# K's transposes by DMA instead of TensorE, from the second sequence on

## The reference

```python
h = layernorm(x, ln_g, ln_b)
q = (h @ Wq).reshape(B, S, H, DH).transpose(0, 2, 1, 3)
k = (h @ Wk).reshape(B, S, H, DH).transpose(0, 2, 1, 3)
q = l2norm(q) * q_scale
k = l2norm(k) * k_scale
logits = jnp.einsum('bhid,bhjd->bhij', q, k) * QK_SCALE
logits = jnp.where(causal, logits, NEG_INF)
attn = jax.nn.softmax(logits, axis=-1)
```

## Time and profile before

| | |
|---|---|
| median of 3 runs | 1125.51 us (1121.51 to 1126.7) |
| the profiled execution's own time | 1120.17 us |
| its span, first to last instruction | 1118.4 us |
| mean granted TensorE clock | 0.986 |
| busy: PE / DVE / ACT / POOL | 96% / 86% / 70% / 25% |
| share of the chain that ended last: PE / DVE / ACT | 89% / 4% / 2% |

### The profile page before, as it was taken

How to read it: one execution, slowest core, us unless ns; L and a number is a source line. 1 busy time by engine, 2 the same in 40 slices (tenths; PEclk the granted TensorE clock), 3 DMA queues, 4 the chain that set the end, 5 groups by cost and what they waited for, 6 DMA issues and landing times.

```text
span 1118.4 us, 27576 instructions
## 1 busy us (share of the span) xinstructions
PE 1075.0 (96%) x10435; PEld 912.2 (82%) x10435; DVE 959.6 (86%) x2543; ACT 778.9 (70%) x1772; POOL 277.7 (25%) x328
## 2 busy tenths in 40 slices
PE   4877999999999999999999999999999999999997
PEld 1664888888888888888888888888888888888897
DVE  8988798898988989898898989889898888988763
ACT  5873948668595876859677594867759587685653
POOL 2340314224031231404123140412403132140200
PEclk9995999999999999999999999999999999999999
DMA  7010000000000000000000000000000000000000
GB/s 210 7 39 10 2 11 7 1 16 1 11 7 11 6 2 16 1 11 6 6 11 2 11 7 11 6 1 16 2 11 6 11 7 6 6 6 1 7 2 10
DMA packets 18722, 14.60 MB, mean 13 GB/s; under 512 B 2408, under 2 KB 16160, under 8 KB 18592
## 3 DMA queue, kind: packets, MB, share of 16 engines
q1 hardware_dynamic: 17680, 12.76, 3.8%
q10 hardware_dynamic: 912, 0.09, 0.1%
HBM read 10.75 MB, written 2.10 MB: 11 GB/s over the span
## 4 chain that ended last, share of the span: by engine, by line
PE 89%; DVE 4%; issue 3%; ACT 2%; POOL 1%; SPq 0%; DMA 0%; POOLq 0%; DVEq 0%; ACTq 0%
PE O L565 19%; PE O L468 14%; PE S L484 5%; PE U L547 5%; PE U L548 5%; PE U L549 5%; PE J L382 5%; PE S L449 4%; PE J L343 4%; PE U L449 4%; PE S L404 4%; PE J L344 3%; PE J L345 3%; PE S L400 3%; PE O L475 2%
## 5 line engine op out<-in xcount | busy, mean ns | idle before, releaser
L777 ACT ACTIVATE hid<-U,b1c 128x256 f32<-128x256 f32 x512 | 200.5, 474 | 174.8 <-PE U L549 174.7
L565 PE MATMUL O<-w2s,hid 128*128 128x128 f32 x2048 | 251.1, 276 | 0.0
L565 PEld LDWEIGHTS O<-w2s,hid 128*128 128x128 f32 x2048 | 238.6, 192 | 2.9
L928 POOL TENSOR_SCALAR_AFFINE_SELECT P<-P 128x512 f32<-128x512 f32 x128 | 85.0, 664 | 618.6 <-ACT P L750 618.5
L468 PEld LDWEIGHTS O<-Vx,P 128*128 128x128 f32 x1536 | 188.0, 192 | 30.2 <-issue 14.3
L468 PE MATMUL O<-Vx,P 128*128 128x66 f32 x1536 | 188.6, 273 | 3.6 <-POOL P L928 2.0
L1198 DVE TENSOR_TENSOR_SCAN st<-aexp,u 128x256 f32<-128x256 f32 x256 | 178.8, 698 | 0.4 <-issue 0.3
L920 POOL TENSOR_TENSOR raw<-raw,nr 128x512 f32<-128x512 f32 x124 | 132.8, 1097 | 134.9 <-DVE nr L1066 134.9
L1208 DVE SCALAR_TENSOR_TENSOR y<-st,bc,y 128x256 f32<-128x256 f32 x240 | 133.5, 556 | 8.5
L547 PE MATMUL U<-h2h,w1h 128*128 128x256 f16 x480 | 130.9, 273 | 0.0
L549 PE MATMUL U<-h2h,w1l 128*128 128x256 f16 x480 | 130.9, 273 | 0.0
(11 more groups left out here) (204 smaller groups left out, 2048.0 us busy)
## 6 DMA issues: line engine op xcount, KB each, us to landing
xin<-in_L_attn_x SPq DMA_DIRECT2D x16, 128.0 KB, 2.1
xres<-in_L_attn_x SPq DMA_DIRECT2D x16, 128.0 KB, 2.3
hid<-in_L_ffn_w SPq DMA_DIRECT2D x2, 1024.0 KB, 6.5
out_dram<-fin SPq DMA_DIRECT2D x16, 128.0 KB, 1.8
raw<-in_L_ffn_Wq SPq DMA_DIRECT2D x1, 512.0 KB, 4.7
raw<-in_L_ffn_Wk SPq DMA_DIRECT2D x1, 512.0 KB, 6.4
raw<-in_L_ffn_Wv SPq DMA_DIRECT2D x1, 512.0 KB, 7.4
wos<-in_L_ffn_Wo SPq DMA_DIRECT2D x1, 512.0 KB, 11.4
```

The costliest lines, as they stand in the source:

```text
L565: last = mm(O[e % 2][:, t * P:(t + 1) * P], hid[:, e % 2, m, t * P:(t + 1) * P], w2s[:, e * FC + m, :], start=(m == 0), stop=(m == FC - 1))
L777: fn(hid[:, e % 2, f % FC, :], U[q % 2][:, m * SEQ:(m + 1) * SEQ], ACT.Gelu_apprx_tanh, bias=b1c[:, f:f + 1], scale=1.0 / WS).then_inc(gel ...
```

## The change

From the second sequence on, K is split into its halves in token order, into two new tiles `Kh` and `Kl`, and the halves are turned from there by DMA transposes of 128x128 that SyncE issues, into `KTh` and `KTl`. Q goes the old way. Sequence 0 is left as it was. The core of the diff:

```diff
+KT = 2 * T * 16
...
+        Kh = sb("Kh", [P, T, HD], F16)
+        Kl = sb("Kl", [P, T, HD], F16)
...
+        kt_high = [sem(f"kt_high{q}") for q in range(NP // 2)]
+        kt_low = [sem(f"kt_low{q}") for q in range(NP // 2)]
...
+        def turn_bank(s, n):
+            return J[n % 2] if s == 0 else J[n // 2 % 2]
...
+            def turn_keys(s, quarter, low):
+                if quarter == 0 and not low:
+                    sp.wait_ge(st_ready, s * NP)
+                if low:
+                    sp.wait_ge(t_lo, s * NL + 2 * quarter + 2)
+                else:
+                    sp.wait_ge(t_hi, s * NL + 2 * quarter + 2)
+                src, dst, done = ((Kl, KTl, kt_low) if low else (Kh, KTh, kt_high))
+                for p in (2 * quarter, 2 * quarter + 1):
+                    for t in range(T):
+                        sp.dma_start_transpose(dst[:, p, t * P:(t + 1) * P], src[:, t, p * P:(p + 1) * P]
+                                               ).then_inc(done[quarter], 16)
...
                 if older:
                     store_out(i - 2)
+                if new:
+                    for quarter in range(NP // 2):
+                        turn_keys(i + 1, quarter, False)
+                        turn_keys(i + 1, quarter, True)
...
             def scores_for_max(s, p):
-                pe.wait_ge(t_hi, s * NL + 2 * (p // 2) + 2)
+                if s == 0:
+                    pe.wait_ge(t_hi, 2 * (p // 2) + 2)
+                else:
+                    pe.wait_ge(t_hi, s * NL + 2 * (p // 2) + 1)
+                    pe.wait_ge(kt_high[p // 2], s * KT)
...
+                if p % 2 == 0 and s > 0:
+                    pe.wait_ge(kt_low[p // 2], s * KT)
...
                     if new and m in TURN_AT:
                         turn_qk(i + 1, TURN_AT[m])
-                        turn_qk(i + 1, TURN_AT[m] + 1)
...
             def high(s, n):
...
+                elif s > 0:
+                    half, c0 = quarter // 2, quarter % 2 * 2 * P
+                    act.wait_ge(unit, s * NJ + half * 4 + 4)
+                    from_one(act, kt_high[quarter], (s - 1) * KT)
+                    fn(Kh[:, :, p * P:(p + 2) * P], raw[:, 4 * half + 1:4 * half + 4:2, c0:c0 + 2 * P], ACT.Copy
+                       ).then_inc(t_hi, 1)
...
             def low(s, n):
...
+                elif s > 0:
+                    half, c0 = quarter // 2, quarter % 2 * 2 * P
+                    from_one(dve, kt_low[quarter], (s - 1) * KT)
+                    V.tensor_tensor(Kl[:, :, p * P:(p + 2) * P], raw[:, 4 * half + 1:4 * half + 4:2, c0:c0 + 2 * P],
+                                    Kh[:, :, p * P:(p + 2) * P], ALU.subtract).then_inc(t_lo, 1)
```

More of the change, by code:

```diff
@@ L252, in y_bank, with turned @@
             return S2[:, 1, 0:SEQ] if s == LAST else O[0][:, 0:SEQ]
+        def turned(s, n):
+            return n + 1 if s == 0 else NL + (s - 1) * (NP // 2) + n // 2 + 1
+        def turn_bank(s, n):
+            return J[n % 2] if s == 0 else J[n // 2 % 2]
         def step_bank(s):
@@ L372, in turn_qk @@
                 pe.wait_ge(unit, s * NJ + half * 4 + kind * 2 + 2)
-                if n < 2 and s > 0:
-                    pe.wait_ge(v_done, s * 2 * T + 3 + n)
+                if s > 0 and n < 4:
+                    pe.wait_ge(v_done, s * 2 * T + 3 + n // 2)
+                elif s > 0:
+                    pe.wait_ge(t_lo, s * NL + n - 3)
                 elif n < 2:
@@ L381, in turn_qk @@
                     for t in range(T):
-                        last = tr(J[n % 2][:, (a * T + t) * P:(a * T + t + 1) * P],
+                        last = tr(turn_bank(s, n)[:, (a * T + t) * P:(a * T + t + 1) * P],
                                   raw[:, chunk(t, kind, half), c0:c0 + P], ident[:, :])
@@ L718, in high @@
                 quarter, kind = divmod(n, 2)
-                act.wait_ge(t_ready, s * NL + n + 1)
                 p = 2 * quarter
                 if kind == 0:
-                    fn(QTh[:, p, :], J[n % 2][:, 0:SEQ], ACT.Copy, scale=wcol[:, p:p + 1])
-                    fn(QTh[:, p + 1, :], J[n % 2][:, SEQ:2 * SEQ], ACT.Copy, scale=wcol[:, p + 1:p + 2]
+                    act.wait_ge(t_ready, turned(s, n))
+                    bank = turn_bank(s, n)
+                    fn(QTh[:, p, :], bank[:, 0:SEQ], ACT.Copy, scale=wcol[:, p:p + 1])
+                    fn(QTh[:, p + 1, :], bank[:, SEQ:2 * SEQ], ACT.Copy, scale=wcol[:, p + 1:p + 2]
+                       ).then_inc(t_hi, 1)
[4 more added lines that the diff above has]
+                    fn(Kh[:, :, p * P:(p + 2) * P], raw[:, 4 * half + 1:4 * half + 4:2, c0:c0 + 2 * P], ACT.Copy
                        ).then_inc(t_hi, 1)
                 else:
+                    act.wait_ge(t_ready, turned(s, n))
                     fn(KTh[:, p:p + 2, :].rearrange("p a q -> p (a q)"), J[n % 2][:, :], ACT.Copy).then_inc(t_hi, 1)
@@ L1083, in low @@
                 if kind == 0:
-                    V.scalar_tensor_tensor(QTl[:, p, :], J[n % 2][:, 0:SEQ], wcol[:, p:p + 1], QTh[:, p, :],
+                    bank = turn_bank(s, n)
+                    V.scalar_tensor_tensor(QTl[:, p, :], bank[:, 0:SEQ], wcol[:, p:p + 1], QTh[:, p, :],
                                            ALU.mult, ALU.subtract)
-                    V.scalar_tensor_tensor(QTl[:, p + 1, :], J[n % 2][:, SEQ:2 * SEQ], wcol[:, p + 1:p + 2],
+                    V.scalar_tensor_tensor(QTl[:, p + 1, :], bank[:, SEQ:2 * SEQ], wcol[:, p + 1:p + 2],
                                            QTh[:, p + 1, :], ALU.mult, ALU.subtract).then_inc(t_lo, 1)
+                elif s > 0:
+                    half, c0 = quarter // 2, quarter % 2 * 2 * P
+                    from_one(dve, kt_low[quarter], (s - 1) * KT)
+                    V.tensor_tensor(Kl[:, :, p * P:(p + 2) * P], raw[:, 4 * half + 1:4 * half + 4:2, c0:c0 + 2 * P],
+                                    Kh[:, :, p * P:(p + 2) * P], ALU.subtract).then_inc(t_lo, 1)
                 else:
```

## The result

| | before | after |
|---|---|---|
| median of 4 runs each, us | 1123.85 (1121.51 to 1126.7) | 1282.48 (1277.02 to 1286.63) |
| the profiled execution's own time, us | 1120.17 | 1277.02 |
| its span, us | 1118.4 | 1275.3 |
| mean granted TensorE clock | 0.986 | 0.938 |

The kernel became slower: the ratio of the times is 1.1407, with a 95% interval from 1.1376 to 1.1439. The forecast was 1252 us, in a range from 1145 to 1370.

A forecast was written before the change was run, and what follows sets the result against it. TensorE, busy 96% of the span, was taken to bound the kernel. Waits for K's high halves add 8.55 us in fourteen bodies and 12.3 in body 0, 132.0 on 1120.2: 1252 us, range 1145 to 1370.

The forecast's parts named there:

- this cover: Input load behind all 32 transposes lands near 576.7; VectorE reads it at 580.5 in the longer body, covered by 3.8 us.
- the sum: Fourteen bodies grow 8.55 us each, 119.7, plus 12.3 in body 0: 132.0 us on top of 1120.2.
- d: Spacing between two DMA transposes on SyncE's queue, bounded by 0.47 and 2.1 us, taken at 1.3 us.
- L: Landing time of a DMA transpose from issue, taken at 2.1 us from a load of the input x.
- From the fourth quarter's product to the next body's first issue: TensorE's stretch after the last quarter's product: nothing shortened, as it holds no K transposes and is dense.
- the second rival: Waits also cost TensorE's clock: 2.3 us lost after the fourth wait, 15 bodies, 35 us, 1287 us; chance 0.12.
- signs of being wrong: In the profile: spacing near 0.5 us, one long wait, VectorE waiting for input x, or clock below 1 between waits.
- swallowed by the next waits: On TensorE, work lost to half clock after the first three waits is absorbed by the next wait; after the fourth it stays.
- The ceiling: K's half of TensorE's transposes, 1.84 us a body; were all gained, fifteen bodies give back 27.6 us.
- The rival that ends on the other side: Transposes as cheap to issue as plain DMAs, d = 0.47: a body shortens by 0.9 us, 1108 us; faster, chance 0.07.

The follow-up runs named there:

- idle turns: Kernel before, TensorE's K turns kept, plus 32 unawaited DMA transposes a body of a weight into a spare tile, input load moved behind third quarter: 1122.2 us.
- two orders: Two reorderings of SyncE's queue in the kernel after: highs-first, 1357.42 us, and highs-then-load, 1179.82 us.
- highs-first: Kernel after with all four high halves of K issued ahead of the four low halves: 1357.42 us.
- two wide: Kernel after with each 128x256 DMA transpose taking the place of two, 16 a body: 1119.09 us.
- one wide: Kernel after with each 128x512 DMA transpose taking the place of four, 8 a body, K's halves laid out quarter by quarter: 1109.96 us.
- highs-then-load: Against the highs-first kernel, the load of xin is moved up between the high and low halves: 1179.82 us.
- kernel without turns: Kernel after without K's DMA transposes and the waits for them, sequences 1 to 15 scored against sequence 0's keys: 1112.37 us.

## Why the prediction was right

**The mechanism.** It came as forecast: SyncE's queue, back to back from K's first copy, TensorE waiting for each quarter's high half. The idle turns and the two orders show that the wait is the cost, and that the queue's order sets it. VectorE never waited for `xin`, as forecast: loaded at 726.51 and landed 2.3 later, it is first read at 734.47, 5.7 us on, where 3.8 were forecast. What comes when this cover is gone is what the highs-first run shows.

**The spacing.** The step that carried the sum was d, bounded by 0.47 and 2.1 us from rows of plain DMAs and taken at 1.3. Measured: 1.27. That it came so close is in part luck. The value is the middle of two rows, and the reason for looking there, that a transpose has more to hand out, does not fit the wide ones: two and four times as much in one instruction held the queue no longer (1.25 and 1.19 us). L was taken at 2.1 and is 2.4. The Trainium skill's 1309 ns for such a transpose (VectorE: DVE Perf Modes, The three transpose paths) agrees to 3%. The other rule of the Trainium skill, that transpose DMAs are as fast as regular ones (Advanced Engine Details and Errata, X-Bar Transpose (TRN2)), holds here for the landing (2.4 us beside 2.3 of the loads of 128 KB) but not for the issue: a load held the queue 0.59 us at 726.51, a transpose about 1.23.

**The size.** The time is 30 us above the forecast; between the profiled executions the difference is 156.9 us where the sum said 132.0. Up to the output of body 1 it is 12.8 us (12.3 forecast for body 0), 1.3 of them a later start of body 0's output, so the rest lies in the other fourteen: 10.3 us each in place of 8.55. Two terms were undersized.

- From the first issue to the fourth quarter's product I had 37.2 us; the mean of fourteen bodies is 38.1. By d and L alone it would be 36.8. The rest is the issues that hold the queue up to 1.1 us longer, one to three in each body: ahead of the fourth quarter's last high half their excess is 1.3 us a body. The forecast had no such term.
- From the fourth quarter's product to the next body's first issue it should have stayed at 37.55 us. It is 37.7 in 7 of the 13 bodies, and 39.3 in the other 6. In those the clock fell after the fourth wait, 0.68 in the windows row above: 1.6 us each, some 10 us in all. This is the second rival, given a chance of 0.12, true in about half of the bodies and at 1.6 us instead of 2.3.

**The long issues.** Issues that held the queue over 0.3 us above the median are 31 in the 480 transposes of the kernel after, 18 in 240 two wide and 8 in 120 one wide, but 38, 40 and 50 in the 480 of the highs-first, highs-then-load and idle kernels. The trace shows what they meet, packets of the queue that the page calls instruction, 82 of 16 KB each:

```profile
q8 instruction: 82, 1.34, 0.4%
```

In the kernel after, each of the 31 had such a packet in flight within its first microsecond, and of the other 449 only 7 had. Two wide it is 18 of 18 beside 9 of 222, one wide 8 of 8 beside 9 of 112. So the long issues go by how many of these packets fall on a queue that is transposing, not by the bytes. No run changed the packets; why one holds the issue up is not shown.

**The clock.** The argument against that rival failed: that waits of 3.4 us and less are too short to cost it, because the one in body 0 was 4.06. The first wait, 3.4 us in twelve of the 14 bodies from body 1 on and 3.6 and 4.2 in the other two, cost it in 12 of them: 5.95 to 6.15 or 8.4 us from the first score product to the second, 4.53 where it was kept. Waits with a clock below 1 between them stand among the prediction's own signs of being wrong, and this sign came (0.76 in the windows row above). At the fourth wait length does not decide it either: 2.29 us lost the clock in one body, 3.30 kept it in another. That a clock lost at the first wait would be swallowed by the next waits was right: the second wait is 0.92 in the body shown, where 1.8 was forecast. In the kernel with one wait alone nothing swallows it, and its bodies take 70.0 us in the mean where one that kept the clock takes 68.3 (not all of that is the clock: in one of them the wait itself was a microsecond longer, 4.39, and four have a third wait of 0.5 to 0.7 us).

**The ceiling.** The text named 27.6 us as what all the saved transposes would be worth, and 12 to 13 as what a cheap queue would leave, 1108 us, since the copy of the output holds the first quarter. The kernel without turns came to 1112.4 and the one-wide kernel to 1110.0, 10.3 and 12.5 us below the kernel before beside them. The rival that ends on the other side had the right sum. Its condition was met by fewer instructions, not by cheaper ones.

## What to carry to other kernels

Count DMA transposes by instruction: here 1.2 to 1.3 us of the issuing queue each, whether 32 or 128 KB. Make few wide ones, and lay the source out so that one covers what a consumer waits for. Read the whole queue behind an edit: putting the urgent half first made the kernel slower until the load behind it was moved too. Before going after a wait that ends a saving early, look at what the engine that ends it does next, since here moving its copy forward only moved the wait.

## What the runs showed of the hardware that I had not expected

- A DMA transpose from SBUF to SBUF held SyncE's queue 1.19 to 1.25 us and landed after 2.4 us at 128x128, 128x256 and 128x512 alike.
- Some transposes held the queue longer (up to 2.69 us in the two-wide kernel). In the kernel after all 31 of them had a packet of the instruction queue q8 in flight in their first microsecond, and 7 of the other 449.
- 480 transposes beside the kernel before, 32 in each of bodies 0 to 14, changed its time by less than 0.3% (0.9973 to 1.0011).
- The same wait of 3.4 us cost TensorE's clock in some bodies and not in others: 4.53, 5.95 to 6.15, or 8.4 us for the same work behind it.
